# A scrap clear behind each indirect gather, and scores and weights moved to PSUM, in a graph attention layer

## What is computed

```
Q, K, V = x @ Wq + bq, x @ Wk + bk, x @ Wv + bv        # per node, as 8 heads of 12
E       = edge_attr @ We + be                          # per edge
score   = exp(clip(sum_d(K[src] * Q[dst] / sqrt(12) * E), -5, 5))
h       = segment_sum(V[src] * score, dst) / (segment_sum(score, dst) + 1e-6)
out     = layernorm(x + h)                             # no scale, no bias
```

## Time and profile before

| what | value |
|---|---|
| median of 3 runs | 1037.03 us (1035.45 to 1042.03) |
| profiled execution, its own time | 1036.28 us |
| its span, first to last instruction | 1034.5 us |
| share of the span in which an engine is busy | PE 72%, DVE 57%, ACT 46%, POOL 74% |
| mean granted TensorE clock | 0.84 of full speed |
| DMA moved over the span | 153.16 MB, mean 148 GB/s |

### The profile page before, as it was taken

The page is one execution under the profiler, slowest core; times in us unless marked ns, Lnnn a source line. Parts: engine busy times, 40 slices in busy tenths (PEclk is TensorE's granted clock), DMA queues, the critical chain, the costliest instruction groups (busy, mean ns, idle before and its releaser), DMA issues.

```text
span 1034.5 us, 12102 instructions
## 1 busy us (share of the span) xinstructions
PE 748.0 (72%) x3375; PEld 433.7 (42%) x3375; DVE 588.1 (57%) x1506; ACT 475.7 (46%) x1021; POOL 764.0 (74%) x790
## 2 busy tenths in 40 slices
PE   5989967568667676777676867756877676677762
PEld 4746534334334343444343434433444443334442
DVE  4449855455556555555556555546564655565554
ACT  2577644344334443435345434536454355436433
POOL 6677777777777777777777777777777777777770
PEclk9999989878888898888788877988878798778875
DMA  9977866655664566555554654564546546545531
GB/s 233 319 180 185 200 157 153 164 148 134 165 154 126 127 154 153 126 135 148 149 127 123 168 139 124 144 163 126 136 125 162 142 124 166 148 123 127 134 85 29
DMA packets 93761, 153.16 MB, mean 148 GB/s; under 512 B 53005, under 2 KB 71631, under 8 KB 88980
## 3 DMA queue, kind: packets, MB, share of 16 engines
q1 hardware_dynamic: 49856, 73.72, 28.8%
q0 software_dynamic: 37008, 75.28, 28.1%
q10 hardware_dynamic: 6822, 3.31, 1.3%
HBM read 142.26 MB, written 9.98 MB: 147 GB/s over the span
## 4 chain that ended last, share of the span: by engine, by line
POOL 55%; issue 19%; DMA 13%; DVE 8%; ACT 2%; PE 1%; SPq 0%; POOLq 0%; DVEq 0%
POOL kv L459 55%; DMA kv<-kv_table,src_idx 11%; DMA q_table<-node_stage 2%; DVE kq L717 2%; DVE score L724 2%; DVE node_stage L699 1%; DVE node_stage L738 1%; DVE qe_t L707 1%; DMA w_all<-biases_in 1%; ACT node_stage L511 1%; ACT node_stage L569 0%; PE ps_eq L878 0%; ACT node_stage L579 0%; DVE clipped L731 0%; DVE node_stage L775 0%
## 5 line engine op out<-in xcount | busy, mean ns | idle before, releaser
L459 POOL DMA_INDIRECT kv<-kv_table,src_idx x750 | 731.9, 976 | 233.0 <-issue 226.0
L558 ACT ACTIVATE node_stage<-clipped 128x32 f32<-128x32 f32 x196 | 44.9, 229 | 494.5 <-DVE clipped L731 494.3
L717 DVE TENSOR_TENSOR kq<-kv,ps_eq_qe 128x384 f32<-128x384 f32 x98 | 54.0, 551 | 212.4 <-DMA kv<-kv_table,src_idx 212.0
L937 PE MATMUL ps_eq<-pick_t,q_win 128*96 128x512 f32 (+1 forms) x262 | 153.0, 669 | 22.8 <-ACT e_t L553 19.4
L930 PE MATMUL ps_eq<-ea,w_all 128*96 128x512 f32 (+1 forms) x262 | 159.5, 694 | 7.0 <-DVE qe_t L707 5.4
L948 PE MATMUL ps_eq_qe<-ident,qe_t 96*128 96x96 f32 x392 | 60.0, 284 | 116.8 <-DVE kq L717 116.8
L717 DVE TENSOR_TENSOR kq<-kv,ps_qe_seg 128x384 f32<-128x384 f32 x98 | 53.7, 548 | 158.7 <-DMA kv<-kv_table,src_idx 158.5
L544 ACT ACTIVATE distance<-rel_bc,neg_part 80x512 bf16<-80x512 bf16 x196 | 138.5, 706 | 2.6 <-issue 2.5
L959 PE MATMUL ps_last<-node_stage 128*104 128x80 f32 x780 | 109.8, 296 | 31.1 <-DVE acc_t L753 31.1
L959 PE MATMUL ps_qe_seg<-node_stage 128*104 128x80 f32 x784 | 104.2, 285 | 31.5 <-DVE acc_t L753 31.4
L547 ACT ACTIVATE pick_t<-distance 80x512 f32<-80x512 bf16 x196 | 123.2, 629 | 6.2
(11 more groups left out here) (84 smaller groups left out, 689.5 us busy)
## 6 DMA issues: line engine op xcount, KB each, us to landing
ea<-ea_t_in SPq DMA_DIRECT2D x49, 768.0 KB, 5.6
rel_bc<-rel_rows_dram SPq DMA_DIRECT2D x49, 320.0 KB, 6.6
kv<-kv_table,src_idx POOLq DMA_INDIRECT x750
q_win<-q_table SPq DMA_DIRECT2D x196, 30.0 KB, 6.2
kv_table<-node_stage SPq DMA_DIRECT2D x5, 960.0 KB, 6.0
x_both<-x_t_in SPq DMA_DIRECT2D x5, 480.0 KB, 12.2
q_table<-node_stage SPq DMA_DIRECT2D x5, 480.0 KB, 7.4
x_both<-x_rows_in ACTq DMA_DIRECT2D x10, 240.0 KB
```

Source lines behind the costliest of these rows:

```text
L459: pool.indirect_dma_start(rows[0:n, :], None, table, bass.IndirectOffsetOnAxis(ap=src_idx[0:n, tile:tile + 1], axis=0)).then_inc(semaphore ...
L717: nc.vector.tensor_tensor(kq[:, group % 2, 0:n, :], kv[:, slot, 0:n, 0:DIM], ps_qe[group % 2][:, 0:n * DIM].rearrange("p (t d) -> p t d", ...
L937: nc.tensor.matmul(ps_eq[(2 * group + 1) % 3][0:DIM, 0:n], q_win[:, slot, :], pick_t[:, group % 3, 0:n], start=True, stop=True).then_inc(e ...
```

## The change

- Behind each `gather`, GpSimd clears a scrap tile `spacer` of 128 partitions by 128 floats, which nothing reads, and increments `e_space`. From the second one on it waits first until the clear before has ended.
- The scores and the window numbers (`window_iota`) move from SBUF to the PSUM bank that was `ps_node`. ScalarE computes the exponentials twice: once into a PSUM tile `weight`, and once into `msg` as before. `weigh_v` multiplies by `weight` instead of by `msg`'s columns. `make_pick` waits for `e_weight`.
- `ps_node` lies now beside the segment sums in their two banks; `segment_sums` waits for `divide` where both would use the bank.
- EARLY is 9 instead of 8 groups.
- The last node steps have two and three tiles instead of four and one; node steps come one group earlier in `divide` and behind it; steps 0 to 10 run inside the loop, and two behind it.

```diff
-EARLY = 8
+EARLY = 9
...
+LAST_TILES = 3
+FIRST_TILES = [*range(0, NODE_TILES - LAST_TILES, FINAL_TILES), NODE_TILES - LAST_TILES, NODE_TILES]
+STEPS = len(FIRST_TILES) - 1
...
-LAG_TRANSPOSE, LAG_DIVIDE, LAG_SQUARE, LAG_RSTD, LAG_NORMALISE = 7, 8, 9, 10, 11
-STREAMED_STEPS = sum(after + LAG_NORMALISE < GROUPS for after in FINISHED_AFTER)
+LAG_TRANSPOSE, LAG_DIVIDE, LAG_SQUARE, LAG_RSTD, LAG_NORMALISE = 7, 7, 8, 9, 10
+STREAMED_STEPS = sum(after + LAG_NORMALISE < GROUPS + ADDED for after in FINISHED_AFTER)
...
-        window_iota = iota[:, 0:WINDOW]
+        window_iota = ps_dve[:, 0:WINDOW]
+        score = ps_dve[:, 2 * P:2 * P + 2 * GROUP_TILES * HEADS].rearrange(
+            "p (b t h) -> p b t h", b=2, t=GROUP_TILES)
+        weight = ps_dve[:, 3 * P:3 * P + GROUP_TILES * HEADS].rearrange("p (t h) -> p t h", t=GROUP_TILES)
+        ps_node = [bank[:, WINDOW:WINDOW + FINAL_TILES * SUMS] for bank in ps_seg]
...
+            def space(tile):
+                if tile:
+                    pool.wait_ge(e_space, tile)
+                nc.gpsimd.memset(spacer[:], 0.0).then_inc(e_space, 1)
+
             pool.wait_ge(l_src_early, 16)
             for group in range(EARLY):
                 for t in range(GROUP_TILES):
                     gather(kv[:, group, t, 0:DIM], x_rows, group, t, e_kv[group])
+                    space(group * GROUP_TILES + t)
...
                     for t in range(tiles_of(group)):
                         gather(kv[:, slot, t, :], kv_table, group, t, e_kv[slot])
+                        space(group * GROUP_TILES + t)
...
                 act.wait_ge(e_clip, group + 1)
+                nc.scalar.activation(weight[:, 0:n, :], clipped[:, group % 2, 0:n, :], ACT.Exp).then_inc(e_weight, 1)
                 nc.scalar.activation(msg[:, group % MSG_RING, 0:n, DIM:SUMS], clipped[:, group % 2, 0:n, :], ACT.Exp
...
+                dve.wait_ge(e_weight, group + 1)
                 rel = rel_f[:, group * GROUP_TILES:group * GROUP_TILES + n]
...
-                    m[:, :, DIM:SUMS].unsqueeze(3).to_broadcast([P, n, HEADS, HEAD_DIM]), ALU.mult
+                    weight[:, 0:n, :].unsqueeze(3).to_broadcast([P, n, HEADS, HEAD_DIM]), ALU.mult
...
-            def segment_sums(group):
+            def segment_sums(group, streamed):
...
+                for step in steps_at(group, 2 + 2, streamed):
+                    pe.wait_ge(f_div, step + 1)
```

More of the change, by code:

```diff
@@ L64 @@
 X_PARTS = 10
-X_PARTS_FROM, X_PARTS_EVERY = 2 * EARLY, 4
+X_PARTS_FROM, X_PARTS_EVERY = 16, 4
 SPAN = 512
@@ L71 @@
 STEP_NODES = FINAL_TILES * P
-STEPS = -(-NODE_TILES // FINAL_TILES)
+LAST_TILES = 3
+FIRST_TILES = [*range(0, NODE_TILES - LAST_TILES, FINAL_TILES), NODE_TILES - LAST_TILES, NODE_TILES]
+STEPS = len(FIRST_TILES) - 1
 FINAL_RING = 3
@@ L78 @@
 IN_RANGE = "the least of node numbers below N_NODES, and of N_NODES where edges are padded"
-FINISHED_AFTER = [math.ceil(GROUPS * math.sqrt((step + 1) * STEP_NODES / N_NODES)) + 1 for step in range(STEPS - 1)]
+FINISHED_AFTER = [math.ceil(GROUPS * math.sqrt(first * P / N_NODES)) + 1 for first in FIRST_TILES[1:STEPS]]
 TURNED, WEIGHED, SUMMED, ADDED = 2, 3, 5, 5
-LAG_TRANSPOSE, LAG_DIVIDE, LAG_SQUARE, LAG_RSTD, LAG_NORMALISE = 7, 8, 9, 10, 11
-STREAMED_STEPS = sum(after + LAG_NORMALISE < GROUPS for after in FINISHED_AFTER)
+LAG_TRANSPOSE, LAG_DIVIDE, LAG_SQUARE, LAG_RSTD, LAG_NORMALISE = 7, 7, 8, 9, 10
+STREAMED_STEPS = sum(after + LAG_NORMALISE < GROUPS + ADDED for after in FINISHED_AFTER)
 def tiles_of(group):
@@ L99, in steps_at, with node_bank @@
     return [s for s in range(STREAMED_STEPS) if FINISHED_AFTER[s] + lag == group] if streamed else []
+def node_bank(step, streamed):
+    return (FINISHED_AFTER[step] if streamed and step < STREAMED_STEPS else step) % 2
 def steps_left(streamed):
@@ L106, in tiles_in @@
 def tiles_in(step):
-    return min(FINAL_TILES, NODE_TILES - step * FINAL_TILES)
+    return FIRST_TILES[step + 1] - FIRST_TILES[step]
 def stores_of(step):
-    first, n = step * FINAL_TILES, tiles_in(step)
+    first, n = FIRST_TILES[step], tiles_in(step)
     whole = min(n, N_NODES // P - first)
@@ L124, in build @@
     assert N_NODES + WINDOW <= ACC_NODES and N_NODES + P <= TABLE_ROWS + 1
+    assert all(FIRST_TILES[step] == step * FINAL_TILES for step in range(STREAMED_STEPS + 1))
     assert X_PARTS_FROM + X_PARTS * X_PARTS_EVERY < FINISHED_AFTER[0]
@@ L127, in build @@
     assert PICK_RING > ADDED - WEIGHED and MSG_RING >= ADDED - TURNED and QE_RING > TURNED
+    assert SUMS * FINAL_TILES + WINDOW <= 512 and LAG_TRANSPOSE == SUMMED + 2
     assert EARLY < KV_RING and tiles_of(EARLY) == GROUP_TILES
@@ L206, in build @@
         pick_t = sb("pick_t", [P, 3, GROUP], F32)
-        score = sb("score", [P, 2, GROUP_TILES, HEADS], F32)
         kq = sb("kq", [P, 2, GROUP_TILES, DIM], F32)
@@ L214, in build @@
         rows_f = acc_t[0:PAIRS, 0:2 * GROUP].rearrange("p (j e) -> p j e", j=2)
+        spacer = sb("spacer", [P, P], F32)
         g_src = sb("g_src", [P, GROUP_TILES], U32)
@@ L236, in build @@
         banks = [pair[:, i, :] for pair in ps_table for i in range(2)]
-        ps_eq, ps_qe, ps_seg, ps_node = banks[0:3], banks[3:5], banks[5:7], banks[7]
+        ps_eq, ps_qe, ps_seg, ps_dve = banks[0:3], banks[3:5], banks[5:7], banks[7]
         ps_early_kv, ps_early_t = banks[0:4], banks[6:8]
-        window_iota = iota[:, 0:WINDOW]
+        window_iota = ps_dve[:, 0:WINDOW]
[3 more added lines that the diff above has]
+        ps_node = [bank[:, WINDOW:WINDOW + FINAL_TILES * SUMS] for bank in ps_seg]
         l_x = [sem(f"l_x{i}") for i in range(STAGES)]
@@ L261, in build @@
         c_wq = sem("c_wq")
+        c_window = sem("c_window")
         t_mm = sem("t_mm")
@@ L288, in build @@
         e_clip = sem("e_clip")
+        e_weight = sem("e_weight")
         e_exp = sem("e_exp")
@@ L292, in build @@
         e_acc = sem("e_acc")
+        e_space = sem("e_space")
         g_free = sem("g_free")
@@ L405, in store_result @@
                 for tile, n, rows in stores_of(step):
-                    first = (step * FINAL_TILES + tile) * P
+                    first = (FIRST_TILES[step] + tile) * P
                     sp.dma_start(out[first:first + (n - 1) * P + rows, :].rearrange("(t p) d -> p t d", p=rows),
@@ L570, in squares @@
                                          accum_out=var[:, s, t:t + 1]).then_inc(f_var, 1)
-                act.wait_ge(f_var, step * FINAL_TILES + n)
+                act.wait_ge(f_var, FIRST_TILES[step + 1])
                 nc.scalar.activation(std[:, s, 0:n], var[:, s, 0:n], ACT.Sqrt,
@@ L594, in windowed @@
                     copy_features(group)
-                for group in range(GROUPS):
+                for group in range(GROUPS + ADDED - TURNED):
                     if group + TURNED + 2 < GROUPS:
@@ L599, in windowed @@
                         copy_features(group + TURNED + 1)
-                    exponentials(group)
+                    if group < GROUPS:
+                        exponentials(group)
                     part, between = divmod(group - X_PARTS_FROM, X_PARTS_EVERY)
@@ L688, in _ @@
             dve.wait_ge(x_copy, EARLY)
+            nc.vector.tensor_copy(window_iota, iota[:, 0:WINDOW]).then_inc(c_window, 1)
             dve.wait_ge(c_acc, 1)
+            dve.wait_ge(c_window, 1)
             path = path_of(dve)
@@ L757, in heads, with divide @@
                 return a.rearrange("p t (h d) -> p t h d", h=HEADS)
-            def divide(step):
-                first, n, s = step * FINAL_TILES, tiles_in(step), step % FINAL_RING
-                sums = ps_node[:, 0:n * SUMS].rearrange("p (t c) -> p t c", t=n)
+            def divide(step, streamed):
+                first, n, s = FIRST_TILES[step], tiles_in(step), step % FINAL_RING
+                sums = ps_node[node_bank(step, streamed)][:, 0:n * SUMS].rearrange("p (t c) -> p t c", t=n)
                 dve.wait_ge(f_tr, step + 1)
@@ L788, in rescale, with finish_nodes @@
                                         ).then_inc(f_shift, 1)
-            def finish_nodes(steps):
+            def finish_nodes(steps, streamed):
                 dve.wait_ge(l_xn, 16 * X_PARTS)
                 for step in steps:
-                    divide(step)
+                    divide(step, streamed)
                     if step > steps[0]:
@@ L818, in windowed @@
                     for step in steps_at(group, LAG_DIVIDE, streamed):
-                        divide(step)
+                        divide(step, streamed)
                     for step in steps_at(group, LAG_RSTD, streamed):
                         rescale(step)
-                finish_nodes(steps_left(streamed))
+                finish_nodes(steps_left(streamed), streamed)
             def general():
@@ L862, in general @@
                 dve.sem_inc(g_acc, 1)
-                finish_nodes(range(STEPS))
+                finish_nodes(range(STEPS), False)
             by_path(dve, path, windowed, general)
```

(26 more changed lines are left out.)

## The result

The changed kernel takes 1077.1 us (median of 4 runs, 1075.75 to 1077.43), the kernel before 1036.36 beside it. The ratio is 1.0379, 95% interval 1.034 to 1.0417: 3.8% slower, where I forecast 1011 and faster. The profiled execution has a span of 1075.6 us.

A forecast was written before the change was run, and what follows sets the result against it. GpSimd's gathers, one every 1.25 us, were taken to bound the kernel. From 1036.3 us, 20, 4.1 and 1.5 came off and 0 was added for clears: 1010.7, about 1011 at the median; 8-in-10 range 925 to 1120.

The forecast's parts named there:

- Scores, weights and window numbers in PSUM: VectorE operands: at most one SBUF input no longer holds up GpSimd's gathers; 20 us saved, bounds 0 and 21.
- the long gathers: GpSimd gathers of 1.07 or 1.30 us instead of 0.94, starting under a VectorE instruction with two SBUF inputs.
- The second exponential and the new waits: ScalarE's extra 45 us fit its idle time; waits of `make_pick` and TensorE cost nothing, or a few tenths at the end.
- Nine early groups: Before the tables' end: four more gathers fill GpSimd's 4.65 us idle; gain 4.1 us, between 3.5 and 4.4.
- The last steps: Kernel's tail: finer steps save some 4.6 us, squares and table loads delay the last group 3.1; net -1.5 us.
- The clears: GpSimd, behind each gather: a 0.20 us clear fits in the 0.30 us idle there, so it costs 0.
- the pause: GpSimd between two gathers: 0.30 us with nothing recorded, taken as handling of the next gather, not the gather's own work.
- The bounds of -0.17 and +0.44: Clear's cost per gather on GpSimd, in us: from -133 us to +344 us over the kernel.
- hidden: Clear fits in the idle 0.30 us between gathers; step stays 1.25 us, time 1011 us; chance 0.38.
- in the pause's place: Rival: clear replaces the idle time between gathers; step 1.15 us or less, 933 us; chance 0.29.
- paid in full: Rival: idle time is the gather's own work, clear queues behind it; step 1.38 us or more, 1113 us; chance 0.27.
- the slower case: Clears paid in full on GpSimd; decides from 0.033 us per clear, using up the other parts' 26 us; chance 0.27.

The follow-up runs named there:

- e9: Changed kernel without the clears, with scores, weights and window numbers all read from SBUF again, second exponential kept: 1030.33 us, ratio 0.9945 to the kernel before.
- e1: Changed kernel without the 782 clears, their signals and waits, all else kept: 1009.45 us, ratio 0.9757 to the kernel before.
- e4: Kernel before the change with the same 128-column clears added behind each gather, nothing else changed: 1106.46 us, ratio 1.0695 to the kernel before.
- e10: Changed kernel without the clears, with eight early groups instead of nine: 1013.26 us, ratio 0.9779 to the kernel before.
- e12: Changed kernel without the clears, squares of the loop's last node step moved behind the last exponentials: 1006.51 us, ratio 0.9707 to the kernel before.
- e7: Changed kernel without the clears, with the scores back in SBUF: 1010.33 us, ratio 0.9752 to the kernel before.

## Why the prediction was wrong

**What bounds the kernel** was right: GpSimd's step sets the time in every run.

**Scores, weights and window numbers in PSUM**: right in mechanism and size. 20 us forecast; e9 against e1 shows 0.9945 - 0.9757, or 19.5 us, and the excess goes from 19.7 to 0.6. `clip` has no part in it, and beside the clears the long gathers would have cost 27 (e4).

**The second exponential and the new waits** at nothing: right by e1, which has them and is 2.4% faster than before. No run leaves out the second exponential alone; e9, which keeps it and has the PSUM operands undone, is about 6 us faster than before (0.0055), and the early group and the last steps make up some 5 of them, so little is left for it to cost. VectorE waited 4.7 us in all for `e_weight` in the changed kernel.

**Nine early groups**: 4.1 forecast, 3.3 in the traces of e10 and e1. In the changed kernel itself nearly all of it was lost: the first gather from the table came at 56.14, and with eight groups and clears (e4) the same gather comes at 51.06 + 4 x 1.337 = 56.41. The early clears had filled the idle time that the ninth group was to use. I had costed this part as if the clears didn't exist.

**The last steps**: -1.5 forecast; the tail went from 25.0 (1034.5 - 1009.49) to 23.3 us (1075.6 - 1052.34), -1.7. The 3.1 us on the last group's path were there (the pause between the last two exponentials went from 1.75 to 4.94, by 3.2), and e12 takes them off.

**The clears** at 0: this is the step that failed. "A clear of 0.20 has room in the 0.30 that are there" took the pause for one piece that a clear can fill. It measured +0.083 us a gather, 65 us: 0.13 of the pause gives room, and 0.17 comes again behind every clear of 24 columns or more. The bounds of -0.17 and +0.44 held it. None of the three cases had it: hidden (1.25), in the pause's place (1.15) and paid in full (1.38 and more) treated the pause as all or nothing, and 1.337 lies between the first and the last. The point given for the slower case was right: it decides from 0.033 us per clear.

**The chances** leaned to faster, since I counted two ways of gaining against one of paying. That the clear alone takes 0.20 and that nothing in the trace of before showed a gather starting sooner for any reason spoke for the slow side; the rival in the pause's place had no row of its own and didn't deserve 0.29. The Trainium skill's "GPSIMD Engine Reference", section 2.1, has each core begin an instruction when it has ended its share of the one before, from which I had the pair of cores pay for every clear in series. The traces agree beyond the first dozen columns or so: 0.74 to 0.83 ns a column. They don't for the first, which are free.

The range held the time, 925 to 1120 us, but it was wide enough to hold nearly anything.

## What to carry to other kernels

An idle gap of an engine between two instructions that bound the kernel is not free room: put in the smallest instruction first, then a longer one, and look at start to start. On an engine that makes gathers, it pays to look at which instructions of VectorE run where a long gather starts, and to give those an operand in PSUM. A step that needs another activation table goes behind the last step of the chain that everything waits for, not in front of it.

## What I had not expected of the hardware

- A clear of 128 partitions by one column, 0.12 us long, with signal and wait, behind each of 782 gathers costs nothing: 1009.63 against 1009.45 us. The idle time behind it shrinks from 0.30 to 0.19 us.
- The step from gather to gather is 1.251 us whether there is no clear or one of a column, and the idle time behind clears of 24, 128 and 256 columns is the same 0.17 us. What the engine does in it stays open. Clears of 128 columns without signal and wait, on one tile, were not tried.
- A tensor-tensor instruction with two SBUF inputs makes a gather that starts under it longer even where the second input is four values broadcast, 12.9 us over the kernel. The clip of 128x32 from SBUF to SBUF does not (excess 0.5 us against 0.6 with the scores in PSUM).
- The clip is the one that waits: 61 of 61 that start 0.53 to 0.73 us into a gather end with that gather (e7), and none of 65 does with the scores in PSUM (e1).
- The same long gathers cost 20 us without clears between the gathers and 27 us with them (e4), since more gathers then start just behind the start of `weigh_v`.
